# Causal mask added by a float32r matmul, and the last attention stage written out per batch

## What is computed

```python
x = x + xattn(layernorm(x), ctx, ctx, w_q, w_k, w_v, w_o)
x = x + ffn(layernorm(x), ...)
# xattn: 16 heads of 16 features, causal mask, softmax
scores = einsum('bhqd,bhkd->bhqk', q, k) / sqrt(16)
scores = where(tril, scores, -inf)
attn   = einsum('bhqk,bhkd->bhqd', softmax(scores), v)
# ffn: three trees (q, k, v) of depth 4; each token goes to one of 16 leaves
cur = 2 * cur + 1 + (score >= 0)        # four times
out = relu(x @ w1[leaf] + b1[leaf]) @ w2[leaf] + b2[leaf]
# then one plain attention of width 256 over the three outputs
attn = softmax(q @ k.T / 16);  result = attn @ v
```

## Time and profile before

| | us |
|---|---|
| median of 3 runs (lowest, highest) | 778.2 (775.58, 781.82) |
| the profiled execution, its device time | 776.24 |
| its span, first to last instruction | 774.5 |
| PE matmuls busy | 676.1 (87%) |
| PE weight loads busy (PEld) | 533.3 (69%) |
| VectorE (DVE) busy | 448.2 (58%) |
| GpSimd (POOL) busy | 339.0 (44%) |
| ScalarE (ACT) busy | 329.5 (43%) |
| mean granted TensorE clock | 0.916 of 2.4 GHz |

### The profile page before, as it was taken

How to read it: one execution, slowest core, us unless ns; L and a number is a source line. 1 busy time by engine, 2 the same in 40 slices (tenths; PEclk the granted TensorE clock), 3 DMA queues, 4 the chain that set the end, 5 groups by cost and what they waited for, 6 DMA issues and landing times.

```text
span 774.5 us, 15967 instructions
## 1 busy us (share of the span) xinstructions
PE 676.1 (87%) x4977; PEld 533.3 (69%) x4977; DVE 448.2 (58%) x1313; ACT 329.5 (43%) x625; POOL 339.0 (44%) x558
## 2 busy tenths in 40 slices
PE   2475999999999999999999978189979988969997
PEld 1354777788787887888777756167657666658896
DVE  2543456688877887888778455743323323316664
ACT  1011344444444444444443343057757766733331
POOL 2200223245664556555655266750035636643440
PEclk9675798999999999999999678679999999979999
DMA  3779676687868777777866532489988989887883
GB/s 100 225 215 183 210 215 179 190 255 236 260 195 233 239 248 228 213 248 231 260 195 212 166 112 96 150 268 315 327 260 256 306 266 289 278 299 215 265 277 101
DMA packets 164183, 174.57 MB, mean 225 GB/s; under 512 B 15973, under 2 KB 153749, under 8 KB 163989
## 3 DMA queue, kind: packets, MB, share of 16 engines
q1 hardware_dynamic: 152229, 146.91, 61.9%
q0 software_dynamic: 9216, 25.18, 11.0%
q10 hardware_dynamic: 2672, 1.67, 0.8%
HBM read 89.28 MB, written 75.50 MB: 213 GB/s over the span
## 4 chain that ended last, share of the span: by engine, by line
PE 54%; SPq 17%; DMA 12%; issue 8%; ACT 3%; DVE 2%; POOL 1%; another core or an unknown queue 1%; ACTq 1%; DVEq 0%; POOLq 0%
SPq L287 9%; PE banks L632 8%; DMA parts_dram<-k_lo 5%; PE banks L426 5%; PE banks L438 5%; PE banks L623 5%; PE banks L470 4%; DMA k<-parts_dram 3%; PE banks L612 3%; PE banks L442 3%; PE banks L454 3%; PE banks L675 3%; PE banks L696 2%; SPq L294 2%; PE banks L550 2%
## 5 line engine op out<-in xcount | busy, mean ns | idle before, releaser
L1201 POOL TENSOR_SCALAR_AFFINE_SELECT pt<-pt 128x256 f32<-128x256 f32 x256 | 99.5, 412 | 200.3 <-ACT pt L727 196.2
L931 DVE TENSOR_REDUCE mneg<-banks 128x2 f32<-128x512 f32 (+1 forms) x256 | 130.3, 550 | 91.1 <-PE banks L442 70.9
L727 ACT ACTIVATE pt<-banks 128x768 f32<-128x768 f32 x128 | 103.8, 811 | 147.3 <-PE banks L455 115.6
L1088 DVE COPY wb<-wl 128x385 f32 x144 | 59.1, 412 | 116.2 <-issue 54.2
L1214 POOL DMA_INDIRECT xs_dram<-xn2s,place x96 | 95.4, 994 | 27.1 <-issue 21.6
L438 PE MATMUL banks<-k,q 64*128 64x256 f32 x256 | 82.8, 373 | 18.3 <-DVE mneg L931 9.1
L454 PE MATMUL banks<-q,k 66*128 66x256 f32 x256 | 81.1, 368 | 9.6 <-DMA q<-m_lo 5.3
L632 PE MATMUL banks<-wb,hT 128*128 128x256 f32 x288 | 82.8, 410 | 7.5 <-issue 3.8
L438 PEld LDWEIGHTS banks<-k,q 64*128 64x128 f32 x256 | 50.0, 195 | 44.9 <-issue 21.5
L632 PEld LDWEIGHTS banks<-wb,hT 128*128 128x128 f32 x288 | 49.6, 192 | 25.3 <-issue 14.6
L1250 POOL DMA_INDIRECT q_all<-ys_dram,place x32 | 31.5, 984 | 73.8 <-DMA ys_dram<-yb 54.5
(11 more groups left out here) (146 smaller groups left out, 1238.6 us busy)
## 6 DMA issues: line engine op xcount, KB each, us to landing
xb<-xs_dram SPq DMA_DIRECT2D x72, 256.0 KB
ys_dram<-yb SPq DMA_DIRECT2D x72, 256.0 KB
k<-parts_dram SPq DMA_DIRECT2D x128, 128.0 KB
xs_dram<-zero SPq DMA_DIRECT2D x45, 256.0 KB
q<-parts_dram SPq DMA_DIRECT2D x64, 128.0 KB
q<-parts_dram SPq DMA_DIRECT2D x128, 64.0 KB
xs_dram<-zero SPq DMA_DIRECT2D x18, 384.0 KB, 4.3
xt<-x SPq DMA_DIRECT2D x16, 256.0 KB, 4.0
```

Source lines behind the costliest of these rows:

```text
L727: nc.scalar.activation(pt[:, 2 * p:2 * p + 2, :], ST_BANKS[:, :, 0:S + P], ACT.Exp, scale=SC).then_inc(exp_sb, 1)
L931: last = nc.vector.tensor_reduce(mneg[1 - u][:, t, 2 * j:2 * j + 2], S_BANKS[:, :, cols], axis=AX.X, op=ALU.max, negate=True)
L1201: last = pool.affine_select(out=dg, in_=dg, compare_op=ALU.is_ge, fill=0.0, base=0, pattern=[[0, 2], [1, P]], channel_multiplier=-1)
```

## The change

**Mask.** The identity and the mask get float32r copies, `identr` and `mask2`; the mask is built in a float32 tile `mask` first. The matmul of line 442 (429 after the change) takes them. There is one constant more to wait for.

**Last stage.** `qr`, `kr`, `pidx` and their semaphores are gone. PE transposes straight from `q_all` and `k_all`, and waits for `q_in` and `k_in` itself before the first batch; SP no longer copies rows and no longer waits for them; GpSimd gathers V with `place` itself. The loop over the middle batches is written out on all five engines.

```diff
-        identb = sb("identb", [P, P], BF)
-        mask2 = sb("mask2", [P, 2 * P], BF)
+        identr = sb("identr", [P, P], FR)
+        mask = sb("mask", [P, 2 * P])
+        mask2 = sb("mask2", [P, 2 * P], FR)
...
-        NCONST = 12
+        NCONST = 13
...
             sp.wait_ge(y_sb, TREES * PAIRB)
-            sp.wait_ge(q_in, 16 * NB * T)
-            sp.wait_ge(k_in, 16 * NB * T)
             for u in range(U):
-                load_qk(0, u)
                 load_x1r(0, u)
-            with sp.Fori(1, NB // U) as i:
+            for i in range(1, NB // U):
                 for u in range(U):
-                    load_qk(i, u)
                     store_final(i - 1, u)
                     load_x1r(i, u)
...
-                    last = mm(S_BANKS[:, e, P:S + P], identb[:], mask2[:], start=False, stop=True)
+                    last = mm(S_BANKS[:, e, P:S + P], identr[:], mask2[:], start=False, stop=True)
...
             def transposes(i, u):
                 b = i * U + u
-                pe.wait_ge(qk_in[u], 32 * (i + 1))
-                for ps, src, done, free in ((banks[0], qr[u], tq_ps, qT_sb), (banks[1], kr[u], tk_ps, kT_sb)):
+                if b == 0:
+                    pe.wait_ge(q_in, 16 * NB * T)
+                    pe.wait_ge(k_in, 16 * NB * T)
+                for ps, src, done, free in ((banks[0], q_all, tq_ps, qT_sb), (banks[1], k_all, tk_ps, kT_sb)):
                     ge(pe, free, b)
                     for t in range(T):
                         for c in range(C):
                             last = nc.tensor.transpose(ps[:, c * S + t * P:c * S + t * P + P],
-                                                       src[:, t, c * P:c * P + P], ident[:])
+                                                       src[:, b, t * D + c * P:t * D + c * P + P], ident[:])
...
-            with pe.Fori(1, NB // U - 1) as i:
+            for i in range(1, NB // U - 1):
                 finals(i, True)
...
             gp.wait_ge(consts, 11)
-            pool.tensor_copy(identb[:], ident[:]).then_inc(consts, 1)
+            pool.tensor_copy(identr[:], ident[:]).then_inc(consts, 1)
+            pool.tensor_copy(mask2[:], mask[:]).then_inc(consts, 1)
...
-                pool.tensor_copy(pidx[u][:], place[:, bass.ds(b * T * TREES, T * TREES)]).then_inc(idx_cp, 1)
-                gp.wait_ge(idx_cp, b + 1)
-                apart(gp)
                 for t in range(T):
-                    m = t * TREES + TREES - 1
+                    m = (b * T + t) * TREES + TREES - 1
                     gp.indirect_dma_start(vr[u][:, t, :], None, ys_dram[TREES - 1],
-                                          bass.IndirectOffsetOnAxis(ap=pidx[u][:, m:m + 1], axis=0)
+                                          bass.IndirectOffsetOnAxis(ap=place[:, m:m + 1], axis=0)
                                           ).then_inc(v_in[u], 16)
```

More of the change, by code:

```diff
@@ L154, in build @@
         ffn.close()
-        pidx = [sb(f"pidx{i}", [P, T * TREES], I32) for i in range(U)]
-        qr, kr, vr = ([sb(f"{n}{i}", [P, T, D]) for i in range(U)] for n in ("qr", "kr", "vr"))
+        vr = [sb(f"vr{i}", [P, T, D]) for i in range(U)]
         qT, kT = ([sb(f"{n}{i}", [P, C * S]) for i in range(2)] for n in ("qT", "kT"))
@@ L192, in build @@
         q_in, k_in = sem("q_in"), sem("k_in")
-        qk_in, v_in = sems("qk_in", U), sems("v_in", U)
-        (idx_cp, tq_ps, qT_sb, tk_ps, kT_sb, s2_ps, m2_sb, mb2_sb, e2_sb, rs2_sb, pT_ps, pT_sb, o_ps,
-         res_sb) = (sem(n) for n in ("idx_cp tq_ps qT_sb tk_ps kT_sb s2_ps m2_sb mb2_sb e2_sb rs2_sb "
+        v_in = sems("v_in", U)
+        (tq_ps, qT_sb, tk_ps, kT_sb, s2_ps, m2_sb, mb2_sb, e2_sb, rs2_sb, pT_ps, pT_sb, o_ps,
+         res_sb) = (sem(n) for n in ("tq_ps qT_sb tk_ps kT_sb s2_ps m2_sb mb2_sb e2_sb rs2_sb "
                                      "pT_ps pT_sb o_ps res_sb").split())
@@ L380, in rows @@
                 return ap[bass.ds(b * S, S), :].rearrange("(t p) d -> p t d", p=P)
[L382 to L389, removed]
             def load_x1r(i, u):
@@ L852, in _ @@
             finals(0, True)
-            with act.Fori(1, NB // U - 1) as i:
+            for i in range(1, NB // U - 1):
                 finals(i, True)
@@ L1146, in _ @@
             finals(0, True)
-            with v.Fori(1, NB // U - 1) as i:
+            for i in range(1, NB // U - 1):
                 finals(i, True)
@@ L1154, in _ @@
             pool = nc.gpsimd
-            for tile, value in ((ident, 0.0), (mask2, 0.0), (trib, 1.0), (onesb, 1.0), (mhalf, -0.5), (zero, 0.0),
+            for tile, value in ((ident, 0.0), (mask, 0.0), (trib, 1.0), (onesb, 1.0), (mhalf, -0.5), (zero, 0.0),
                                 (vp[0], 1.0), (vp[1], 1.0)):
@@ L1160, in _ @@
                                pattern=[[-1, P]], channel_multiplier=1).then_inc(consts, 1)
-            m2v = mask2[:].rearrange("p (e k) -> p e k", e=2)
+            m2v = mask[:].rearrange("p (e k) -> p e k", e=2)
             pool.affine_select(out=m2v, in_=m2v, compare_op=ALU.is_ge, fill=NEG, base=0,
@@ L1259, in gather @@
                 ge(gp, v_in[u], 32 * i)
-                pool.tensor_copy(pidx[u][:], place[:, bass.ds(b * T * TREES, T * TREES)]).then_inc(idx_cp, 1)
-                gp.wait_ge(idx_cp, b + 1)
-                apart(gp)
                 for t in range(T):
-                    m = t * TREES + TREES - 1
+                    m = (b * T + t) * TREES + TREES - 1
                     gp.indirect_dma_start(vr[u][:, t, :], None, ys_dram[TREES - 1],
-                                          bass.IndirectOffsetOnAxis(ap=pidx[u][:, m:m + 1], axis=0)
+                                          bass.IndirectOffsetOnAxis(ap=place[:, m:m + 1], axis=0)
                                           ).then_inc(v_in[u], 16)
-            for u in range(U):
-                gather(0, u)
-            with gp.Fori(1, NB // U) as i:
+            for i in range(NB // U):
                 for u in range(U):
```

## The result

The changed kernel takes 784.0 us (median of 20 runs, 776.04 to 798.75) against 777.71 us of before in the same comparison (median of 20). The ratio is 1.0084, 95% interval 1.006 to 1.0109: 0.8% slower. The profiled execution took 784.39 us with a span of 782.5 us.

The account below looks back on a forecast made before the run. The attention stage was taken as bound by TensorE's stream of loads and matmuls. From 776.24 us, +10.5 for the mask and -5.3 for the last stage gave 781.4 us, 0.7% more; range 768 to 790.

Parts of the forecast that it names:

- part 2: Last stage: transposing straight from q_all and k_all, without the copies, saves 5.3 us (range -7 to -0.4).
- Part 1: Attention stage: the mask matmul with float32r operands costs 10.5 us in all (range -4.4 to +22).
- The step on the gap: Attention pairs: the 0.15 us between last score matmul and mask comes from changed tile height, not type, and stays.
- The float32r rhythm: Attention pairs: the next load comes 0.22 us after the mask's first instead of 0.12, +0.10 us a pair.
- The upper bound of +22 us: Attention pairs: the mask matmul streams like a float32 record of 256 columns, +0.22 us a pair.
- The constants: Start of the kernel: GpSimd's float32 mask fill and extra copy take some 0.4 us but cost nothing.
- The clock: Start of the last stage: shorter PE idling may keep the clock up, at most -2.8 us; half taken, -1.5 us.
- the rival by the clock: Attention, 100 to 420 us: the later mask causes one more stretch at 1.2 GHz, 7.9 us, giving 789.3 us; chance 0.14.
- the unrolled loops add no work: Last stage: written-out loops execute the same instructions, less branches and register arithmetic that are hidden; no cost.
- The type theory: Attention pairs: the gap belongs to the type change, so float32r saves 0.04 us a pair, giving 766.5 us; chance 0.17.
- the quick float32r load: Attention pairs: the identity's float32r load is as quick as bf16, so the mask change costs nothing, 770.9 us; chance 0.08.
- part 2 gains only its gap: Last stage: only the gap at 714.79 is gained, 0.4 us, as V or k gathers hold PE; 786.3 us, chance 0.06.

Follow-up runs that it names:

- mask_only: The kernel before with only the mask matmul's operands changed to float32r; 782.0 us, 1.0127 of before.
- k66_bf16: The kernel before with 66 rows in place of 64 in the score matmuls, bf16 mask kept, computation no longer the reference's; 1.0153 of before.
- unroll_only: The kernel before, copies of q, k and indices kept, with all five loops of the last stage written out; 0.9905 of before.
- after_again: The changed kernel itself, unchanged, measured again beside the single-part runs; 787.05 us, 1.0188 of before.
- stage_only: The changed kernel with the mask's operands back in bfloat16, so only the last stage differs from before; 769.19 us, 0.9948, repeated on another chip at 0.9891.

## Why the prediction was right

It said 781.4 us, 0.7% more than the profiled execution of before; measured was 0.84% more. The two terms were there, with opposite signs, and the mechanism of each is the one that was named. That the total fits to 0.2% is in part luck: two sizes inside part 2 were off and offset each other, and the intervals of the single parts are several microseconds wide. The profiled execution itself was 784.39 us, 3 us above the forecast: stage 1 had grown by 7.8 us and not by 10.5, the leaf layers by 4.4 us, for which I had nothing, and the last stage had lost 4.2 us and not 5.3.

**Part 1: +10.5 us said, 9.8 us measured (mask_only, 5.6 to 14).** The step on the gap held in both halves: the load stayed behind L439 (0.15 us), and `k66_bf16` showed that it is the height that holds it. The float32r rhythm laid on the mask's loads gave 0.22 us from the mask's load to the next; the trace has 0.23. The load of the identity takes 188 ns, as the other float32r loads. The starts lie 0.15 us apart with the change of height and 0.07 us without it. This agrees with the drain at a change of tiling mode that the Trainium skill names ("TensorEngine Tiling (Array Packing)", Key Properties); the runs show the gap and what it depends on, not a drain as such. The undisturbed batch, from one transpose of the maxima to the next, grew from 24.8 to 25.7 us, 0.11 us a pair. Over twelve batches of the middle the profiles have 307.7, 307.9 and 308.7 us with float32r and 298.2 to 302.0 us in nine with bf16 (mean 299.5): 8.6 us more instead of 12 x 0.9 = 10.8, because the bf16 versions lose some 2 us in waits for k and the maxima which the slower PE doesn't see. I had put 1.0 us for that. The upper bound of +22 us was added up too low: 0.22 us for 110 pairs are 24 us.

**The constants:** nothing, as said. The first mask matmul stood at 33.5 us in one profile of the changed kernel and at 32.8 us in the other; before at 32.7 and 33.1.

**Part 2: -5.3 us said, -4.0 us measured on the one chip (-7.6 to -0.5), -8.2 on the other (-13.3 to -3.3).** Two sizes were off and they offset each other. The clock: I took half of 2.8 us for lack of knowing; over the 16 us behind the last leaf copy the clock was 1.00 in every profile of a version without the copies and 0.68 or 0.79 in every one with them, so the whole is gained. The load of transfers alone doesn't lower it: from 722 to 762 us before it was 1.00 at a DMA share of 0.84. Nor does the length of a wait decide alone, as the rival by the clock had it: at 701.04 PE had waited 1.64 us in the changed kernel and kept 1.00. From the last leaf copy's end to the first value matmuls it is 9.6 us (694.53 to 704.13) against 16.0 us (682.28 to 698.27): -6.4 us, where I had -4.9. `unroll_only` keeps the copies and has the wait and the slow scores again (15.5 us to the value matmuls), so it is the removed copies and not the written-out code that gain this:

```profile
664.62 0.63 PE L664 MATMUL banks<-ident,qr 128*128 128x128 f32 x4 [4.33 <-DMA kr<-k_all]
...
666.87 3.75 PE L675 MATMUL banks<-kT,qT 128*128 128x256 f32 x8 [0.88 <-DVE kT L1105]
```
And the stall, which I did not have among the costs ("the unrolled loops add no work"): it gives back 2.7 us in the changed kernel's profile, measured as the 7.45 us between the first two batches' value matmuls (704.13 to 711.58) against 4.77 us in the steady batches. In `after_again` it is 2.0 us, and in `stage_only`, where the clock fell behind it, the last stage is 4.3 us longer than without a stall.

**The rivals.** The type theory (0.17) and the quick float32r load (0.08) are refuted. The extra stretch at half clock (0.14) did not come: the clock was 1.00 from 125 to 415 us in every profile of both kernels. Behind 420 us both have such stretches, in other places from profile to profile; the changed kernel's first has none before 450 us (before: 0.50 from 430 to 440) and 0.51 from 460 to 470. That part 2 gains only its gap (0.06) is refuted too; no matmul waited for V. The first gather, though, came 3.45 us behind the last leaf copy (694.53 to 697.98) and not the 2.3 us of the sum (682.28 to 684.6); before it was 3.3. It waited for the last store of y, so that leaving out the index copy did not bring it forward.

## What to carry to other kernels

Where TensorE is bound by its stream of loads, ask of an operand's type what its weight load costs behind the load before it, not only what the matmul streams: the next load came 0.12 us behind the first of two bf16 loads and 0.23 us behind the first of two float32r loads, and over 128 pairs the kernel became 9.8 us slower. Look for the height of the tiles before blaming a type for a gap: two rows more in a matmul removed it. And a copy that only stages data for one reader can cost the reader's clock as well as its own latency; two such edits of opposite sign are best measured apart, since here one hid most of the other.

## What was not expected of the hardware

- Three engines stalled for 0.8 to 3.5 us and went on within 0.2 us of each other, released by what the profile calls "remote", in the same place of the last stage in three profiles. Waits with this end stand in the leaf layers of all six profiles where that stage took 175 to 181 us, and in none of the eight where it took 154 to 159 us.
- The same kernel before took 775, 758 and 756 us (medians) on three chips; the leaf layers, which lean on transfers, took 159.4 us on the last against 175.3 us in the first profile, while twelve middle batches of the attention stage took 299.0 and 302.0 us.
- Two comparisons of one kernel in different groups can differ by more than their intervals (1.0084 and 1.0188 for the changed kernel), so an interval of one chip is not the whole uncertainty.
